# Attention and expert MLP on one core: another slot plan for the attention stage (turning point, projections, loads and low parts moved)

## The chip, the core and the metric

The kernel runs on one core of a Trainium2 chip, in one launch. The metric is the device time in microseconds of one execution. Engines: TensorE (PE), VectorE (DVE), ScalarE (ACT), GpSimd (POOL), and SyncE (SP), which here only issues DMAs. Each of them runs its own list of instructions in the order written; semaphores tie the lists together.

## The reference

`x` is 8 x 512 x 512 in float32. Two layers are added to it, one after the other:

```
query = seq2 + b_self;  key = concat(seq1 + b_prev, seq2 + b_self);  value = concat(seq1, seq2)
q, k, v = query @ Wq + bq, key @ Wk + bk, value @ Wv + bv        # 16 heads of 32
score_prev = mask(q . k[:l1]) * SCALE;  score_self = (q * k[l1:]).sum(-1) * SCALE
weights = softmax(concat(score_prev, score_self))
attn = weights[:-1] @ v[:l1] + weights[-1] * v[l1:]
x = x + (attn @ Wo + bo)                                          # seq1 = x, seq2 = fside
h = gelu(x @ W1 + b1)                                             # 512 -> 2048
x = x + concat(h @ W2 + b2, h @ We[expert] + be[expert])          # 384 + 128 columns
```

Each query sees the 512 keys of the other sequence, masked by a length, and one key of its own.

## The kernel before, in words

The program has two stages. The second is the output projection and the expert MLP; the change does not touch it. The first is the attention, and it runs over 8 batches b with 4 groups g of 4 heads each (128 of the 512 features). The first batch and the last are written out, the six between are one hardware loop.

A product of float32 precision is made of three matmuls: each operand is split into a high part, which the matmul takes as it is, and a low part that holds the rest (`in_hi`, `in_lo`, `w_hi`, `w_lo`). A projection of a group sums 12 such matmuls of 128x512 and is issued in three **thirds** of 4 matmuls. There are four of them per group: k, q, k2 (the key of the query's own position) and v2 (its value), in this order, thus 12 thirds, numbered 0 to 11.

For each group TensorE makes 16 **maximum tiles** (L1148: scores with a query on each partition; VectorE's L832 reduces a tile to a column of maxima), 16 **score tiles** (L1175: the same scores with a key on each partition and the maximum already subtracted; ACT's L639 exponentiates a tile into `p_f`), the sums over keys with the values (**value bursts**, L1188, four matmuls per tile row t of keys) and the denominators (L1197) from sums that POOL makes of the probabilities (L531 and L534, 12 of 128x512 per group).

The work is laid out by hand in 16 **slots** i of each group, one per score tile, and it is staggered. Beside the scores of group g, a slot holds maximum tiles of the next group (`tiles_of_max`) and thirds of the group after next (`thirds_of`). The tables `turn_at`, `in_hi_at` and `in_lo_at` say in which slot (g, i) of batch b an input block j of batch b+1 is transposed on DVE (L806), has its high part made on ACT (L582) and its low part on POOL (L539). Blocks 0 to 3 are of x, 4 to 7 of seq2. The loads that feed them (L317, four DMAs a block, 4 buffers) stand on SP. `turned` has two buffers, so transpose j waits for the low part of block j-2. The k projection of the next batch's group 0 (in group 2) waits for low parts 0 to 3, its q projection for all eight.

In slot 8 of group g TensorE issues the value bursts of tile rows 0 and 1, the denominators of the group before, the own scores (L1157) and the transposition of the maxima (L1165). From there a chain runs to the next group's first tiles: ACT copies the own scores (L622), DVE makes the maximum and its two parts (L840 to L855), SP writes these into the operand of the next group's scores (four DMAs, `stacks<-m_neg`, L339), and then SP writes the **stacks** of the group after next, the operands of its maximum tiles, from the parts of k and q (12 DMAs `stacks<-parts`, L332, three for each of four heads j, with one of the mask at L328 ahead of them where the group is 0 or 1). The first maximum tile in slot 0 of the next group waits for stack 0. SP takes, in each group, in this order: loads (in groups 0 and 1), m_neg of the next group, the stacks of the group after next, the own weights (L348) and the store of the group before (L353).

## Time and profile before

| | before |
|---|---|
| median of 3 runs | 1864.58 us (1861.9 to 1869.23) |
| the profiled execution | 1861.9 us |
| its span, from first to last instruction | 1860.1 us |
| VectorE, ScalarE, GpSimd busy | 49%, 38%, 34% of the span |
| mean granted TensorE clock | 0.968 |
| first stage | up to about 1035 us; one batch of the loop takes about 119 us |
| second stage | about 825 us |

Busy time counts a matmul from its start to the modelled end, so overlapping matmuls count once and short pauses vanish. Where the start times of neighbouring matmuls are farther apart than one matmul needs, TensorE waited. In a timeline, "x2" merges neighbours of one kind, and the brackets at the end tell how long the engine was idle before and who released it.

### The profile page before, as it was taken

The numbers are of one execution on the slowest core, as the hardware profiler recorded it, in microseconds if no ns is written. First come the engines' busy times: TensorE is split into PE (matmuls) and PEld (weight loads), VectorE is DVE, ScalarE is ACT, GpSimd is POOL, SyncE is SP. The second block draws the span as 40 slices with busy tenths as digits, with TensorE's granted clock in tenths as the row PEclk, the third lists the DMA queues.
The fourth block names the chain that finished last, engine by engine and source line by source line (L and its number), as shares of the span: only waits on it lengthen the run. The fifth ranks groups of instructions, "written<-read, shape, count | busy, mean of one in ns | idle before, by whom it ended". The sixth has DMA issues, their size and how long they took to land.

```text
span 1860.1 us, 27844 instructions
## 1 busy us (share of the span) xinstructions
PE 1757.1 (94%) x8384; PEld 1290.8 (69%) x8384; DVE 915.6 (49%) x1399; ACT 709.8 (38%) x1258; POOL 626.6 (34%) x489
## 2 busy tenths in 40 slices
PE   6999999999999999999995899999999999999997
PEld 5666656666566565666651688888888888888886
DVE  4567575775767757667586633222131323132311
ACT  3254353544545435444445242323232323333222
POOL 3167485665765748648375200000000000000000
PEclk8999999999999999999996899999999999999999
DMA  6452434424344335344243321313030312121101
GB/s 139 73 112 70 98 84 103 97 67 101 85 109 81 91 71 116 87 91 94 57 117 121 85 86 23 68 22 70 11 73 17 58 30 52 34 43 47 30 15 23
DMA packets 361052, 132.67 MB, mean 71 GB/s; under 512 B 288202, under 2 KB 328138, under 8 KB 360978
## 3 DMA queue, kind: packets, MB, share of 16 engines
q1 hardware_dynamic: 356370, 129.75, 31.9%
q10 hardware_dynamic: 4608, 2.10, 0.4%
q8 instruction: 26, 0.43, 0.1%
q14 instruction: 48, 0.39, 0.1%
HBM read 62.02 MB, written 18.89 MB: 44 GB/s over the span
## 4 chain that ended last, share of the span: by engine, by line
PE 73%; SPq 7%; issue 6%; DVE 4%; DMA 4%; POOL 4%; ACT 1%; POOLq 0%; DVEq 0%; ACTq 0%
PE ps_proj L1117 10%; PE ps_av L1069 6%; PE ps_av L1071 6%; PE ps_av L1070 6%; PE ps_max L1148 6%; PE ps_av L1188 5%; PE ps_score L1175 3%; DMA stacks<-parts 3%; PE ps_proj L1069 3%; PE ps_max L1071 3%; PE ps_score L1071 3%; PE ps_max L1070 3%; PE ps_score L1070 3%; PE ps_score L1069 3%; PE ps_max L1069 3%
## 5 line engine op out<-in xcount | busy, mean ns | idle before, releaser
L639 ACT ACTIVATE p_f<-ps_score 128x512 f32<-128x512 f32 x512 | 304.9, 599 | 462.2 <-PE ps_score L1175 436.4
L832 DVE TENSOR_REDUCE m_col<-ps_max 128x1 f32<-128x512 f32 x512 | 329.1, 683 | 230.4 <-PE ps_max L1148 229.2
L534 POOL TENSOR_TENSOR p_sum<-p_sum,p_f 128x512 f32<-128x512 f32 x256 | 338.8, 1355 | 2.7 <-ACT p_f L639 2.7
L1002 DVE TENSOR_TENSOR h_lo<-h_f,h_hi 128x512 fp32r<-128x512 f32 x128 | 88.3, 690 | 481.1 <-ACT h_hi L729 480.9
L531 POOL TENSOR_TENSOR p_sum<-p_f 128x512 f32<-128x512 f32 x128 | 162.9, 1304 | 228.1 <-PE ps_av L1197 224.0
L1175 PE MATMUL ps_score<-stacks 99*128 99x512 f32 x512 | 212.3, 425 | 20.0 <-ACT p_f L639 19.9
L1117 PE MATMUL ps_proj<-in_hi,w_hi 128*128 128x512 f32 x512 | 208.6, 407 | 18.0 <-POOL in_lo L539 14.7
L1148 PE MATMUL ps_max<-stacks 97*128 97x512 f32 x512 | 188.1, 435 | 39.0 <-DMA stacks<-parts 28.3
L1117 PE MATMUL ps_proj<-in_lo,w_hi 128*128 128x512 f32 x512 | 206.4, 403 | 0.0
L1117 PE MATMUL ps_proj<-in_hi,w_lo 128*128 128x512 f32 x512 | 205.9, 402 | 0.0
L1069 PE MATMUL ps_av<-y_hi,w_hi 128*128 128x512 f32 x512 | 199.4, 390 | 1.3 <-DVE y_lo L998 1.3
L1071 PE MATMUL ps_av<-y_hi,w_lo 128*128 128x512 f32 x512 | 199.3, 389 | 0.0
L1070 PE MATMUL ps_av<-y_lo,w_hi 128*128 128x512 f32 x512 | 199.2, 389 | 0.0
L727 ACT ACTIVATE h_f<-ps_av,bias 128x512 f32<-128x512 f32 x128 | 88.2, 689 | 242.9 <-PE ps_av L1071 216.8
L1148 PEld LDWEIGHTS ps_max<-stacks 97*128 97x128 f32 x512 | 98.1, 195 | 107.6 <-DVE m_col L832 56.1
L729 ACT ACTIVATE h_hi<-ps_av,bias 128x512 fp32r<-128x512 f32 x128 | 88.2, 689 | 209.0 <-PE ps_max L1071 209.0
L1175 PEld LDWEIGHTS ps_score<-stacks 99*128 99x128 f32 x512 | 98.4, 193 | 84.7 <-issue 38.1
L1188 PE MATMUL ps_av<-p_f,v_st 128*32 128x512 f32 x1024 | 131.3, 627 | 2.6 <-ACT p_f L639 2.6
L1117 PEld LDWEIGHTS ps_proj<-in_hi,w_hi 128*128 128x128 f32 x512 | 100.1, 195 | 41.4 <-POOL in_lo L539 9.1
L1117 PEld LDWEIGHTS ps_proj<-in_lo,w_hi 128*128 128x128 f32 x512 | 99.9, 195 | 21.9
L1117 PEld LDWEIGHTS ps_proj<-in_hi,w_lo 128*128 128x128 f32 x512 | 99.5, 194 | 21.7
L892 DVE RECIPROCAL den<-den 128x128 f32<-128x128 f32 x128 | 112.2, 918 | 0.8
(116 smaller groups left out, 2657.7 us busy)
## 6 DMA issues: line engine op xcount, KB each, us to landing
stacks<-parts SPq DMA_DIRECT2D x384, 128.0 KB
raw<-in_x_dram SPq DMA_DIRECT2D x128, 64.0 KB, 2.2
raw<-in_fside_BxSxS_dram SPq DMA_DIRECT2D x128, 64.0 KB, 2.2
den<-own_scratch SPq DMA_DIRECT2D x128, 64.0 KB, 2.7
attn_scratch<-num SPq DMA_DIRECT2D x32, 256.0 KB, 2.9
x_raw<-in_x_dram SPq DMA_DIRECT2D x128, 64.0 KB, 2.2
a_raw<-attn_scratch SPq DMA_DIRECT2D x32, 256.0 KB, 3.5
we_raw<-in_L_cond_We_dram SPq DMA_DIRECT2D x32, 256.0 KB, 2.7
```

The lines of the kernel that those rows point to most:

```text
L531: pool.tensor_tensor(p_sum[:, j], p_f[:, j], now, ALU.add).then_inc(sum_made, 1)
L534: pool.tensor_tensor(p_sum[:, j], p_sum[:, j], now, ALU.add).then_inc(sum_made, 1)
L639: act.activation(p_f[:, i % FLIGHT], ps_score[i % 2][:, :], ACT.Exp, scale=SCALE).then_inc(p_made, 1)
L832: dve.tensor_reduce(m_col[:, n % C, n // C:n // C + 1], ps_max[n % 2][:, :], AX.X, ALU.max).then_inc(max_made, 1)
L892: dve.reciprocal(den[:, r, at], den[:, r, at]).then_inc(rden_made, 1)
L1069: pe.matmul(ps, left[0], right[0], start=first, stop=False)
L1070: pe.matmul(ps, left[0], right[1], start=False, stop=False)
L1071: return pe.matmul(ps, left[1], right[0], start=False, stop=last)
L1117: mm = pe.matmul(ps, left, right, start=(m == 0), stop=(m == 3 * C - 1))
L1148: pe.matmul(ps_max[n % 2][:, :], q_st[0:KM, r, j, P * t:P * (t + 1)], k_st[0:KM, r, j, :], start=True, stop=True).then_inc(max_mm, 1)
L1175: pe.matmul(ps_score[i % 2][:, :], k_st[0:KS, r, j, P * t:P * (t + 1)], q_st[0:KS, r, j, :], start=True, stop=True).then_inc(score_mm, 1)
L1188: pe.matmul(ps_num[at, :], v_st[:, t, P * g + DH * j:P * g + DH * (j + 1)], p_f[:, i % FLIGHT], start=(t == 0), stop=(t == C - 1)).then_in ...
```

## The change

The slot tables of the attention stage are replaced. The maximum tiles are spread over slots 0 to 9 and not 0 to 7. The value bursts of rows 0 and 1, the denominators and the turning of the maxima, with the steps of ACT and DVE that follow, move from slot 8 to slot 9 (on ACT and DVE from 9 to 10), POOL's sums one slot later too. The thirds stand in other slots. The transposes and the high and low parts of the next batch's inputs stand later in group 1 and group 2. The loads of x move from the start of group 0 to the start of group 1, and those of seq2 from the start of group 1 to behind the m_neg DMAs of group 1, eight ahead of stack 0 and eight ahead of stack 2. In DVE's slot 10 `own_max` now stands ahead of `q_low`. Nothing is computed otherwise, and no instruction is added or taken away.

```diff
@@ -239,15 +239,15 @@
 
         def tiles_of_max(i):
 
-            ends = (2, 4, 6, 8, 10, 12, 14, TILES)
+            ends = (2, 3, 5, 7, 8, 10, 12, 14, 14, TILES)
             return range(ends[i - 1] if i else 0, ends[i]) if i < len(ends) else range(0)
 
 
 
-        turn_at = {(1, 3): (0,), (1, 4): (1,), (1, 7): (2,), (1, 8): (3,), (1, 11): (4,), (1, 12): (5,),
-                   (2, 1): (6,), (2, 2): (7,)}
-        in_hi_at = {(1, 5): (0,), (1, 6): (1,), (1, 8): (2,), (1, 9): (3,), (1, 15): (4,), (2, 0): (5,), (2, 2): (6,), (2, 3): (7,)}
-        in_lo_at = in_hi_at
+        turn_at = {(1, 6): (0,), (1, 7): (1,), (1, 11): (2,), (1, 12): (3,), (1, 14): (4,), (1, 15): (5,),
+                   (2, 2): (6,), (2, 3): (7,)}
+        in_hi_at = {(1, 10): (0,), (1, 11): (1,), (1, 12): (2,), (1, 13): (3,), (2, 0): (4,), (2, 2): (5,), (2, 4): (6,), (2, 5): (7,)}
+        in_lo_at = {(1, 10): (0,), (1, 11): (1,), (1, 12): (2,), (1, 13): (3,), (2, 0): (4,), (2, 2): (5,), (2, 4): (6,), (2, 5): (7,)}
 
 
 
@@ -273,11 +273,11 @@
 
         def thirds_of(g, i):
 
-            slots = ((4, 5, 5, 6, 7, 7, 9, 10, 11, 12, 13, 14), (0, 2, 3, 4, 5, 6, 9, 10, 11, 12, 13, 14),
-                     (0, 2, 3, 5, 6, 7, 9, 10, 11, 12, 13, 15), (0, 2, 3, 4, 5, 6, 9, 10, 11, 12, 13, 15))[g]
+            even = (0, 2, 3, 4, 6, 7, 8, 10, 11, 12, 14, 15)
+            slots = (range(4, TILES), even, (0, 2, 3, 7, 8, 10, 11, 12, 13, 14, 15, 15), even)[g]
             return [n for n, at in enumerate(slots) if at == i]
 
-        k_at, q_at = (6, 4, 4, 4), (8, 7, 8, 7)
+        k_at, q_at = (7, 4, 4, 4), (10, 8, 11, 8)
 
         def first_max(t):
 
@@ -402,8 +402,8 @@
             def batch(b, first, last):
                 for g in range(C):
                     more = not (last and g >= 2)
-                    if g < 2 and not last:
-                        for j in range(C * g, C * (g + 1)):
+                    if g == 1 and not last:
+                        for j in range(C):
                             load(b + 1, j)
                     if last and g == 2:
                         for n in range(6):
@@ -412,6 +412,9 @@
                         maxima(*after(b, g, 1))
                     if more:
                         for j in range(HG):
+                            if g == 1 and j % 2 == 0 and not last:
+                                load(b + 1, C + j)
+                                load(b + 1, C + j + 1)
                             stack(*after(b, g, 2), j)
                     if last and g == 2:
                         for n in range(6, 10):
@@ -557,14 +560,14 @@
                                 in_low(b + 1, j)
                         if i == 8:
                             own_value(b, g)
-                        n = (i + 7) % TILES
-                        if i >= 9:
+                        n = (i + 6) % TILES
+                        if i >= 10:
                             add_probabilities(b, g, 1 + n // HG, n % HG)
                         elif n < SUMS and not (first and g == 0):
                             add_probabilities(*after(b, g, -1), 1 + n // HG, n % HG)
 
             batches(pool, batch)
-            for n in range(7, SUMS):
+            for n in range(6, SUMS):
                 add_probabilities(B - 1, C - 1, 1 + n // HG, n % HG)
 
         @block.scalar
@@ -678,7 +681,7 @@
                     project = not (last and g >= 2)
                     maximum = not (last and g == C - 1)
                     for i in range(TILES):
-                        if i == 9 and maximum:
+                        if i == 10 and maximum:
                             maxima_twice(*nxt)
                             own_row(*nxt)
                         if i == 15 and maximum:
@@ -944,17 +947,18 @@
                                 maximum(*nxt, n)
                         if i == 3 and started:
                             numerator(*after(b, g, -1))
-                        if i == 10 and started:
+                        if i == 11 and started:
                             denominator(*after(b, g, -1))
                         if not last:
                             for j in turn_at.get((g, i), ()):
                                 turn(b + 1, j)
                         if i == k_at[g] + 1 and project:
                             k_low(*nxt2)
+                        if i == 10 and bound:
+                            own_max(*nxt)
                         if i == q_at[g] + 1 and project:
                             q_low(*nxt2)
-                        if i == 9 and bound:
-                            own_max(*nxt)
+                        if i == 10 and bound:
                             m_parts(*nxt)
                             own_less_max(*nxt)
                         if i in (13, 14) and started:
@@ -1235,12 +1239,12 @@
                         if i == 1 and not (first and g == 0):
                             for t in (2, 3):
                                 value_burst(*after(b, g, -1), t)
-                        if i == 8:
+                        if i == 9:
                             for t in (0, 1):
                                 value_burst(b, g, t)
                             if not (first and g == 0):
                                 denominators(*after(b, g, -1))
-                        if bound and i == 8:
+                        if bound and i == 9:
                             own_scores(*nxt)
                             turn_max(*nxt)
             batches(pe, batch)
```

SP in group 1 of batch 0, before: L348 fetches own weights, L317 loads inputs, L339 writes m_neg, L332 the parts into a stack.

```order
L348 DMA den<-own_scratch 32x4x128 x4
L317 DMA raw<-in_fside_BxSxS_dram 32x16x32 x16
L339 DMA stacks<-m_neg 2x4x128 x4
L332 DMA stacks<-parts 32x1024
L332 DMA stacks<-parts 32x2x512 x2
```

And now:

```order
L348 DMA den<-own_scratch 32x4x128 x4
L317 DMA raw<-in_x_dram 32x16x32 x16
L339 DMA stacks<-m_neg 2x4x128 x4
L317 DMA raw<-in_fside_BxSxS_dram 32x16x32 x8
L332 DMA stacks<-parts 32x1024
L332 DMA stacks<-parts 32x2x512 x2
L332 DMA stacks<-parts 32x1024
L332 DMA stacks<-parts 32x2x512 x2
L317 DMA raw<-in_fside_BxSxS_dram 32x16x32 x8
L332 DMA stacks<-parts 32x1024
L332 DMA stacks<-parts 32x2x512 x2
```

Eight loads stand between m_neg and stack 0 and eight between stacks 1 and 2; the sixteen at the start are those of x.

POOL from group 1 to the own value of group 2 in batch 0, before: L539 makes a low part of an input, L522 multiplies an own value, L531 and L534 are the sums of probabilities.

```order
L539 TENSOR_TENSOR in_lo<-turned,in_hi 128x512 x3
L522 TENSOR_TENSOR v<-v,den 128x512
L539 TENSOR_TENSOR in_lo<-turned,in_hi 128x512
L531 TENSOR_TENSOR p_sum<-p_f 128x512 x4
L534 TENSOR_TENSOR p_sum<-p_sum,p_f 128x512 x2
L539 TENSOR_TENSOR in_lo<-turned,in_hi 128x512
L534 TENSOR_TENSOR p_sum<-p_sum,p_f 128x512
L539 TENSOR_TENSOR in_lo<-turned,in_hi 128x512
L534 TENSOR_TENSOR p_sum<-p_sum,p_f 128x512 x2
L539 TENSOR_TENSOR in_lo<-turned,in_hi 128x512
L534 TENSOR_TENSOR p_sum<-p_sum,p_f 128x512
L539 TENSOR_TENSOR in_lo<-turned,in_hi 128x512
```

And now, from the fifth low part on (ahead of these rows stand the own value and, four times in turn, one low part and one first sum, L542 and L534):

```order
L537 TENSOR_TENSOR p_sum<-p_sum,p_f 128x512 x2
L542 TENSOR_TENSOR in_lo<-turned,in_hi 128x512
L537 TENSOR_TENSOR p_sum<-p_sum,p_f 128x512 x2
L542 TENSOR_TENSOR in_lo<-turned,in_hi 128x512
L537 TENSOR_TENSOR p_sum<-p_sum,p_f 128x512 x2
L542 TENSOR_TENSOR in_lo<-turned,in_hi 128x512
L537 TENSOR_TENSOR p_sum<-p_sum,p_f 128x512
L542 TENSOR_TENSOR in_lo<-turned,in_hi 128x512
L537 TENSOR_TENSOR p_sum<-p_sum,p_f 128x512
L525 TENSOR_TENSOR v<-v,den 128x512
```

Before, three low parts stand ahead of the own value and one ahead of the first sum, and between the first sum and the last low part stand 10 sums. Now all eight stand behind the own value, with 11 sums ahead of the last of them.

## Rows read from the trace of the kernel before

**Rows 1.** The page, part 1: busy time, share of the span, instructions.

```profile
PE 1757.1 (94%) x8384; PEld 1290.8 (69%) x8384; DVE 915.6 (49%) x1399; ACT 709.8 (38%) x1258; POOL 626.6 (34%) x489
```

**Rows 2.** Windows: stretch, length, busy time of each engine, PEclk, DMA share, GB/s.

```profile
541.80:660.70 118.90, 112.45 (x593) 74.67 (x592) 81.58 (x129) 54.68 (x105) 77.02 (x61) 0.99 0.41 91
...
1035.40:1860.10 824.70, 811.29 (x3585) 672.01 (x3584) 225.21 (x331) 251.30 (x389) 0.00 (x0) 0.99 0.21 44
```

**Rows 3.** Timeline of PE: start, length, engine, line, operation; two scores a slot apart.

```profile
457.34 0.40 PE L1175 MATMUL ps_score<-stacks 99*128 99x512 f32 x1
...
458.50 0.40 PE L1175 MATMUL ps_score<-stacks 99*128 99x512 f32 x1
```

**Rows 4.** Timeline of PE: the turning points of groups 0, 1, 2, 3 and 0.

```profile
452.26 0.40 PE L1165 MATMUL ps_max<-ident,m_col 128*8 128x128 f32 x8
...
478.22 0.40 PE L1165 MATMUL ps_max<-ident,m_col 128*8 128x128 f32 x8
...
508.62 0.40 PE L1165 MATMUL ps_max<-ident,m_col 128*8 128x128 f32 x8
...
534.07 0.40 PE L1165 MATMUL ps_max<-ident,m_col 128*8 128x128 f32 x8
...
571.17 0.40 PE L1165 MATMUL ps_max<-ident,m_col 128*8 128x128 f32 x8
```

**Rows 5.** The chain that ended last, 534 to 544: start, length, what.

```profile
535.79 0.69 SPq L339
...
539.12 0.57 SPq L332
...
543.09 0.48 PE ps_max L1148
```

**Rows 6.** Timeline of PE, group 2: first maximum tiles, first third of q.

```profile
487.79 0.69 PE L1148 MATMUL ps_max<-stacks 97*128 97x512 f32 x2 [1.54 <-DMA stacks<-parts]
...
499.63 0.50 PE L1117 MATMUL ps_proj<-in_hi,w_hi 128*128 128x512 f32 x1 [1.50 <-POOL in_lo L539]
```

**Rows 7.** Timeline of POOL: the fourth and the eighth low part.

```profile
480.42 1.29 POOL L539 TENSOR_TENSOR in_lo<-turned,in_hi 128x512 fp32r<-128x512 f32 x1
...
498.28 1.29 POOL L539 TENSOR_TENSOR in_lo<-turned,in_hi 128x512 fp32r<-128x512 f32 x1
```

**Rows 8.** Timeline of ACT: a cast to in_hi; the probability behind a turning point.

```profile
473.42 0.61 ACT L582 CAST in_hi<-turned 128x512 fp32r<-128x512 f32 x1
...
509.64 0.60 ACT L639 ACTIVATE p_f<-ps_score 128x512 f32<-128x512 f32 x1 [0.51 <-PE ps_score L1175]
```

**Rows 9.** Timeline of SP: loads and m_neg in group 1, loads in group 0.

```profile
469.90 10.89 SPq L317 DMA_DIRECT2D raw<-in_fside_BxSxS_dram  x16
480.84 2.68 SPq L339 DMA_DIRECT2D stacks<-m_neg  x4
...
551.50 8.45 SPq L317 DMA_DIRECT2D raw<-in_x_dram  x16
```

**Rows 10.** Waits, 300 to 1000: who for whom, us in total, times, longest.

```profile
PEld ps_max L1148 <- DVE m_col L832: 41.1, 118, 0.9
```

**Rows 11.** Lines L810 (q_low) and L898 (normalization): ns min/median/max, first and last start.

```profile
L810 DVE TENSOR_TENSOR parts<-q_f,parts x32: 648/692/716, 37.0 to 952.7; 128x512 fp32r<-128x512 f32 x32
...
L898 DVE TENSOR_TENSOR num<-num,den x32: 692/1526/1753, 126.3 to 1049.2; 128x512 f32<-128x512 f32 x32
```

**Rows 12.** Windows behind two waits: PEclk is the third number from the end.

```profile
499.70:503.50 3.80, 3.80 (x10) 2.98 (x11) 1.26 (x2) 0.60 (x1) 3.57 (x3) 0.55 0.00 0
...
663.90:667.30 3.40, 3.39 (x8) 2.71 (x9) 1.34 (x2) 1.57 (x3) 3.40 (x4) 0.50 0.76 175
```

**Rows 13.** Timelines of POOL and PE at the end of the first stage.

```profile
1016.07 5.87 POOL L531 TENSOR_TENSOR p_sum<-p_f 128x512 f32<-128x512 f32 x4 [14.53 <-PE ps_av L1197]
...
1034.46 1.04 PE L1197 MATMUL ps_av<-p_sum,ones 128*32 128x512 f32 x2 [0.63 <-POOL p_sum L534]
```

## The prediction, made before the changed kernel was run

> **What bounds the kernel now.** Read the share of busy time first, then doubt it: TensorE is busy for 94% of the span [rows 1], but the windows show that the idle part lies in the first stage. One batch of the loop, 541.8 to 660.7, leaves it 6.5 us by the profile's count, while the whole second stage of 825 us loses 13 [rows 2]. The busy share hides more, since matmul records overlap. Two scores that stand a slot apart, with one third of a projection between them, start 1.16 us apart [rows 3]: five matmuls, 0.23 each. A third costs 0.93, a score or a maximum tile 0.23.
>
> The useful mark in this stage is the "turning point": the start of the matmuls L1165, which turn the maxima. Call the one in group g T_g. They stand at 452.26, 478.22, 508.62, 534.07 and 571.17 [rows 4], so the steps are T0 to T1 25.96, T1 to T2 30.40, T2 to T3 25.45, T3 to the next T0 37.10, 118.9 us a batch. From each of them a chain runs that TensorE can't shorten. From 534.07: SyncE starts the four m_neg DMAs at 535.79, starts the stacks of the group after at 539.12, and TensorE's first maximum tile starts at 543.09 [rows 5]: 9.02 us. Beside this chain TensorE has only what stands between the turning point and the end of the group: 7 scores and 6 thirds, 7.2 us. So it waits at each group's start. What stands behind the turning point in a group is free up to about 9 us; what stands ahead of it is paid in full. That is the rule by which I cost the moves.
>
> Group 1 to group 2 is the longest step for its work. The first tile comes at 487.79, 9.57 after T1, with a wait of 1.54; at 499.63 the first third of q waits for POOL's in_lo [rows 6]. POOL had run without a gap from 480.42 until the eighth in_lo ended at 499.57, 15 operations (10 sums, 5 in_lo), 1.277 each [rows 7]. The first three in_lo lay before that, while POOL was idle anyway.
>
> **The change, part by part.** *Turning point one slot later, in every group.* In groups 0, 1 and 3 seven scores and six thirds stood behind it. Now six scores stand there, with six thirds in group 0 (0.23 us less cover), five in groups 1 and 3 (1.16 less), seven in group 2 (0.70 more). What leaves the cover goes ahead of the next mark of its own group, so the step that ends in that group grows: T0 to T1 by 1.16, T2 to T3 by 1.16, T3 to T0 by 0.23.
>
> *in_lo moved behind the marks.* POOL's 8 in_lo now all stand behind the denominators of group 1, with 11 sums among and ahead of the last: 19 operations, not 15. The first can't start before ACT's probability of slot 10, which starts 1.0 after a mark (509.64 against 508.62) and takes 0.60, and a cast to in_hi of 0.61 [rows 8]: T1 + 2.2. So the last in_lo ends at 2.2 + 19 x 1.277 = T1 + 26.5. q's first third is moved from slot 5 to 7 of group 2, but it needs all eight. TensorE's own work up to there is only about 16 us in both kernels, so this wait grows and is not covered. In the kernel before it took 508.62 - 499.63 = 8.99 from that third to T2 [rows 4, 6]; now one third, one score and two maximum tiles fewer stand in between (1.63): 7.4. T1 to T2 is then 33.9 against 30.40: +3.5.
>
> *Loads moved.* SyncE's sixteen loads at the start of group 1 took 10.89 us, because they waited for transposes, and the m_neg DMAs came right behind them, at 480.84, 0.9 later than they otherwise would [rows 5, 9]. That 0.9 goes: the loads at the start of group 1 are now those of x, for which nothing is awaited; such sixteen took 8.45, 0.53 each [rows 9]. But eight loads now stand ahead of stack 0 and eight ahead of stack 2. Stack 0 starts at T1 + 1.72 + 2.7 + 8 x 0.53 + 0.5 of waits = 9.1, and by rows 5 its tile starts 3.97 later: T1 + 13.1, not 9.57. TensorE will stand there some 6.9 us. Does that add to the POOL wait? Both lie between T1 and the same third. From 13.1, the work of slots 0 to 6 and the start of 7 is 9.5, hence 22.6, and stack 2 comes at 4.2 + 1.9 + 4.2 + 1.9 behind the start of stack 0, so tile 8 can't start before about 21.8 and VectorE's reductions of tiles 8 to 11, 0.65 each, with k_low between, bring the third to about 26. POOL's 26.5 is later by little. I charge the larger, not both. Behind the waiting stacks are own_weights and the store of the attention; their users come in slot 8 and later.
>
> *Turns.* Turn j waits for in_lo j-2. On VectorE, behind turns 2 to 5 of group 1, stand the reciprocals, qk, the normalization and the next group's maxima. The in_lo 0 to 3 end at T1 + 3.5, 6.0, 8.6, 11.1, so the normalization ends about 13.8, when the first tile comes anyway: nothing charged, up to 1 us in the upper end.
>
> *Maximum tiles spread.* In slots 5 to 7 of groups 1 and 3 two tiles each now meet a slot without a third, so VectorE (1.3 us for two) is briefly the slower; on the other side the turns leave slots 3 and 4. TensorE's weight loads wait for reductions 118 times in 700 us, 41 us in all [rows 10], but much of it lies beside a running matmul. I take +0.2 for each of groups 1 and 3, between -1.1 (the largest part of such waits in group 1 gone) and +1.
>
> *q_low later.* In group 2 q is cast in slot 11, so q_low ends about T2 + 4.6 on VectorE, and the first parts DMA of stack 0, which waits for it and has a mask DMA of 0.3 ahead, could start at 5.0 [rows 5]. All q_low of the kernel before took 0.65 to 0.72, at a time when POOL is mostly idle; the normalization, also two SBUF inputs, took 0.69 at best and 1.53 in the median, with POOL at its sums [rows 11]. q_low will now meet the sums. The stack comes between 0 and 1.2 later; I take 0.5 on T2 to T3. The Trainium skill, page "SBUF — State Buffer", section "SBUF: two separate sides", says that a VectorE operation with two SBUF inputs and a GpSimd operation exclude each other for the whole instruction. By that rule q_low would always wait for a sum, and the step would be at the upper end, 1.2.
>
> *The clock.* After the wait for in_lo the granted clock was 0.55 over 499.7 to 503.5, the 1.2 GHz level for most of it; in batch 5, after the wait at the start of group 0, it was 0.50 for 663.9 to 667.3 [rows 12]. 3.4 us at half the rate lose 1.7. Group 3 now gives 1.16 less cover before exactly this place, so it will fall more often: +0.3 in the mean, up to 1.6. The loss after in_lo is in the 7.4 already. The Trainium skill, page "TensorE: Matmul & The Clock Gate", section "Part 1: The HAM clock gate", says that idling throttles the array and activity releases it; by it the long stop at group 2's first tile brings a further half-rate stretch. Its 1 to 2 us would lie ahead of POOL's 26.5, where they are hidden.
>
> **The sum.** Per batch 1.36 + 3.5 + (1.16 + 0.2 + 0.5) + (0.23 + 0.3) = 7.3. Loads and group 2's projections exist in seven of the eight batches: 51. In the last batch T0 to T1 adds 1.2. At its end POOL's twelve last sums run from 1016.07 and TensorE's last denominator waits for them [rows 13]; they start one slot later, where scores come every 1.0 us: +1.0. Sum 53.4. The profiled execution took 1861.9 (span 1860.1), so 1915; it was the fastest of the three, the median is 1864.6.
>
> **Rivals.** *Only the later mark costs* (0.12). If POOL's wait and SyncE's stop are hidden, T1 to T2 stays at 30.4: 3.8 x 7 + 2.2 = 29, 1891. For it: POOL is idle a third of each step. Against: its idle time lies before the denominators, and the in_lo were taken out of it.
>
> *The waits add up* (0.11). If the stop at stack 0 and its half-rate stretch push TensorE behind POOL, q's third comes at 29 (T1 to T2 +6.2), q_low takes its 1.2, and every group 0 meets the slow clock (+1.6): about 12 a batch, 1947.
>
> *Faster: the in_lo wait goes* (0.06). q's third is two slots later. If the last in_lo were ready by T1 + 17, the 2.0 us before 499.63, the slow clock behind it (1.4), the 0.9 of SyncE and the 0.7 of cover in group 2 would all be won: 5.1; with group 1's waits for reductions gone too (1.1 instead of +0.2), a batch gets 7.3 - 3.5 - 5.1 - 1.3 = 2.6 shorter, 1846. It decides at T1 + 17, and 19 POOL operations can't be done by then.
>
> *Balance* (0.05). Half of that gain meets the later mark: within 0.5%, which is 9 us and about what a measurement of this kernel can tell from no change.
>
> **How the numbers follow.** My own case has 0.66, with 1903 to 1929 as its range. Its 1915 is the forecast. The lower rival at 1891 is taken in, of the upper one the nearer half: 1889 to 1940. Faster 0.06, same 0.05, slower 0.89.
>
> **What would show it.** In the profile after: the maximum tile at group 2's start about 13 us behind its mark, released by a stack DMA; sixteen x loads without a wait, then eight loads between m_neg and the stacks; POOL without a gap for 24 us in front of q's first third, which waits for in_lo; T0 to T1 about 27.3, T1 to T2 34, T2 to T3 27.3, T3 to T0 37.6; a second stage unchanged at 825. I am wrong if T1 to T2 is at 31 or below, or if steps T0 to T1 and T2 to T3 don't grow by about one slot.

## The result and the profile after

The changed kernel takes 1949.41 us (median of 4 runs, 1937.86 to 1966.88) against 1864.64 before: a ratio of 1.046, with a 95% interval of 1.037 to 1.055. It is slower, as forecast, but by 85 us and not by 53. 1949 lies outside the range of 1889 to 1940. One execution among the experiments below (e1's of 1980.38 us) is over 1.5% slower than the fastest of its kernel, in a slower state of the chip, and is left out of the medians and ratios. In its profiled execution (1959.29 us, span 1957.5) the first line of the page, which answers to [rows 1], reads:

```profile
PE 1794.4 (92%) x8384; PEld 1305.5 (67%) x8384; DVE 937.5 (48%) x1399; ACT 711.9 (36%) x1258; POOL 628.1 (32%) x489
```

TensorE has the same 8384 matmuls and more busy microseconds for them, and VectorE has 22 us more busy time for the same 1399 instructions. Both are explained below. The windows (columns as in [rows 2]) show one batch, from turning point to turning point, and the second stage:

```profile
624.06:753.91 129.85, 116.20 (x600) 75.90 (x592) 83.08 (x128) 54.90 (x104) 77.47 (x60) 0.96 0.38 84
1132.80:1957.50 824.70, 811.27 (x3585) 671.78 (x3584) 225.19 (x331) 251.44 (x389) 0.00 (x0) 0.99 0.21 44
```

The second stage still takes 824.7 us, to the tenth. All of the loss is in the first stage: 129.9 a batch and not 118.9, in a batch without any special event. The turning points of this batch, on TensorE's timeline, answer to [rows 4] (T0, T1, T2, T3 and the next T0; all line numbers are three or four higher now):

```profile
624.06 0.40 PE L1169 MATMUL ps_max<-ident,m_col 128*8 128x128 f32 x8
...
651.47 0.40 PE L1169 MATMUL ps_max<-ident,m_col 128*8 128x128 f32 x8
...
687.68 0.40 PE L1169 MATMUL ps_max<-ident,m_col 128*8 128x128 f32 x8
...
716.49 0.40 PE L1169 MATMUL ps_max<-ident,m_col 128*8 128x128 f32 x8
...
753.91 0.40 PE L1169 MATMUL ps_max<-ident,m_col 128*8 128x128 f32 x8
```

Taken over the whole profiled execution, the steps add up so ("usual" is the value that most batches share; the excess is measured minus before, summed over all such steps):

| step | before | forecast | usual after | others after | excess in all |
|---|---|---|---|---|---|
| T0 to T1 (8) | 25.95 | 27.3 | 27.42 | 31.90 once | 16.9 |
| T1 to T2 (7) | 30.4 | 33.9 | 34.8 to 36.3 | 40.16, 40.87 | 47.7 |
| T2 to T3 (7) | 25.45 | 27.3 | 28.80 | none | 23.4 |
| T3 to T0 (7) | 37.1 or 38.8 | 37.6 | 37.4 or 39.1 to 40.0 | none | 7.3 |
| T1 to T2, last batch | 25.48 | | 27.84 | | 2.4 |

The sum is 97.7, the difference of the two spans 97.4. T1 to T2 holds half of it. The forecast had 53.4 in all; of the 44 beyond it T1 to T2 (with the last batch) makes 26, T2 to T3 10, T0 to T1 6 (4.5 of it in one batch) and T3 to T0 4; the rest of the stage gives 1 to 2 back. Three things happen in the first stage that the prediction priced too low or not at all; the first two lie in T1 to T2.

*First: TensorE stands for stack 0, and then POOL stands too.* In batch 4 the timelines of TensorE, ScalarE and POOL (start, length, engine, line, operation, idle time before it and who ended it) show behind T1 = 651.47:

```profile
664.29 1.19 PE L1152 MATMUL ps_max<-stacks 97*128 97x512 f32 x2 [4.31 <-DMA stacks<-parts]
...
667.98 3.01 PE L1192 MATMUL ps_av<-p_f,v_st 128*32 128x512 f32 x16
...
676.62 0.50 PE L1152 MATMUL ps_max<-stacks 97*128 97x512 f32 x1 [1.23 <-DVE m_col L835]
...
679.16 1.09 PE L1152 MATMUL ps_max<-stacks 97*128 97x512 f32 x2 [0.52 <-DVE m_col L835]
680.33 0.70 PE L1121 MATMUL ps_proj<-in_hi,w_hi 128*128 128x512 f32 x1
```

```profile
672.10 0.61 ACT L585 CAST in_hi<-turned 128x512 fp32r<-128x512 f32 x1
```

```profile
672.79 1.30 POOL L542 TENSOR_TENSOR in_lo<-turned,in_hi 128x512 fp32r<-128x512 f32 x1 [2.58 <-ACT in_hi L585]
...
679.00 1.27 POOL L542 TENSOR_TENSOR in_lo<-turned,in_hi 128x512 fp32r<-128x512 f32 x1
```

The first maximum tile comes at T1 + 12.8 (forecast 13.1). q's first third comes at 680.33, which is T1 + 28.9 and not 26.5. POOL was not gapless: its sixth low part waited 2.58 us for a cast that stands in ScalarE's order behind a probability, and this behind a score that TensorE held back. TensorE's own tiles ahead of the third are done at 680.25, 0.08 before it, so POOL's low part (ended 680.27) and TensorE's chain arrive there together, and both had been held by the stop. From q's third to T2 it is 7.35 (forecast 7.4).

*Second: a VectorE instruction of 7.11 us.* In batch 3 VectorE's timeline reads as follows, with those of POOL and TensorE behind it:

```profile
528.73 0.65 DVE L809 STREAM_TRANSPOSE turned<-raw 128x512 f32<-128x512 f32 x1
529.30 7.11 DVE L901 TENSOR_TENSOR num<-num,den 128x512 f32<-128x512 f32 x1
536.34 1.27 DVE L835 TENSOR_REDUCE m_col<-ps_max 128x1 f32<-128x512 f32 x2
```

```profile
532.12 1.30 POOL L542 TENSOR_TENSOR in_lo<-turned,in_hi 128x512 fp32r<-128x512 f32 x1
533.35 2.52 POOL L537 TENSOR_TENSOR p_sum<-p_sum,p_f 128x512 f32<-128x512 f32 x2
542.84 1.29 POOL L542 TENSOR_TENSOR in_lo<-turned,in_hi 128x512 fp32r<-128x512 f32 x1 [6.98 <-ACT in_hi L585]
```

```profile
537.07 0.79 PE L1152 MATMUL ps_max<-stacks 97*128 97x512 f32 x1 [3.34 <-DVE m_col L835]
```

The normalization reads two tensors of SBUF. POOL had worked without a gap since 519.78 and stopped at 535.87; the normalization ended 0.54 us later, at 536.41. The maxima's reductions stood behind it and TensorE behind them. The same happened in batch 6 (40.87). In the other batches it took 0.90 to 0.98 us, from the same place.

*Third: q_low.* The two lines that answer to [rows 11] (minimum/median/maximum of 32, in ns):

```profile
L813 DVE TENSOR_TENSOR parts<-q_f,parts x32: 680/688/1851, 37.1 to 1047.8; 128x512 fp32r<-128x512 f32 x32
```

```profile
L901 DVE TENSOR_TENSOR num<-num,den x32: 691/1482/7111, 130.8 to 1145.8; 128x512 f32<-128x512 f32 x32
```

In groups 0 and 2, where q_low now meets POOL's sums, it takes 1.55 and 1.65. The median of 688 hides that, as 18 of the 32 still take 0.68 to 0.73.

The clock, in windows around the stop at stack 0 and around q's third (PEclk is the third number from the end):

```profile
663.40:670.20 6.80, 5.91 (x20) 3.08 (x24) 2.75 (x4) 0.60 (x1) 6.80 (x6) 0.50 0.79 146
670.20:680.40 10.20, 8.09 (x34) 4.46 (x26) 8.70 (x15) 5.54 (x10) 7.62 (x8) 1.00 0.48 126
680.50:683.90 3.40, 3.40 (x9) 2.63 (x10) 0.48 (x1) 0.60 (x1) 2.24 (x2) 0.50 0.00 0
```

TensorE is granted the 1.2 GHz level for 6.8 us from the end of the stop on and again for 3.4 us behind q's third. The value burst at 667.98 falls into the first and takes 3.01 us; at the full rate it takes 1.92. In batch 2 the first stretch (397.1 to 404.0) is over when the burst starts at 403.71; the burst takes 2.03, and q's third comes at T1 + 27.9 and not 28.9. In the seven steps T1 to T2 the half rate holds for 85 us in all, where it held for 27 before; in the whole execution it is 207 and 120. Most of TensorE's added busy time is there.

### The profile page after: what moved, and what is told of

The parts are those of the page before. It is cut to its first block, busy times and chain, and to the rows that moved or that the text cites. A ratio compares the mean times of both kernels' runs of the same rounds, so it can differ in the third digit from the quotient of the medians.

```text
span 1957.5 us, 27844 instructions
## 1 busy us (share of the span) xinstructions
PE 1794.4 (92%) x8384; PEld 1305.5 (67%) x8384; DVE 937.5 (48%) x1399; ACT 711.9 (36%) x1258; POOL 628.1 (32%) x489
## 4 chain that ended last, share of the span: by engine, by line
PE 67%; issue 10%; SPq 6%; DMA 5%; DVE 5%; POOL 4%; ACT 1%; POOLq 0%; DVEq 0%; ACTq 0%
PE ps_proj L1121 8%; PE ps_av L1073 6%; PE ps_av L1074 6%; PE ps_av L1075 6%; PE ps_max L1152 5%; PE ps_av L1192 4%; PE ps_proj L1073 3%; DMA stacks<-parts 3%; PE ps_proj L1074 3%; PE ps_proj L1075 3%; PE ps_max L1074 3%; PE ps_score L1074 3%; PE ps_max L1073 3%; PE ps_score L1073 3%; PE ps_max L1075 3%
## 5 line engine op out<-in xcount | busy, mean ns | idle before, releaser
L1152 PE MATMUL ps_max<-stacks 97*128 97x512 f32 x512 | 200.1, 445 | 99.0 <-DMA stacks<-parts 68.7
L534 POOL TENSOR_TENSOR p_sum<-p_f 128x512 f32<-128x512 f32 x128 | 166.9, 1328 | 253.9 <-PE ps_av L1201 251.7
L1179 PE MATMUL ps_score<-stacks 99*128 99x512 f32 x512 | 217.3, 431 | 27.4 <-ACT p_f L642 27.4
L1121 PE MATMUL ps_proj<-in_hi,w_hi 128*128 128x512 f32 x512 | 213.7, 417 | 11.2 <-POOL in_lo L542 7.6
L1192 PE MATMUL ps_av<-p_f,v_st 128*32 128x512 f32 x1024 | 141.7, 669 | 1.8 <-ACT p_f L642 1.8
L542 POOL TENSOR_TENSOR in_lo<-turned,in_hi 128x512 fp32r<-128x512 f32 x64 | 82.1, 1284 | 120.3 <-ACT in_hi L585 120.3
```

What stands on the lines that cost most here:

```text
L534: pool.tensor_tensor(p_sum[:, j], p_f[:, j], now, ALU.add).then_inc(sum_made, 1)
L1121: mm = pe.matmul(ps, left, right, start=(m == 0), stop=(m == 3 * C - 1))
L1152: pe.matmul(ps_max[n % 2][:, :], q_st[0:KM, r, j, P * t:P * (t + 1)], k_st[0:KM, r, j, :], start=True, stop=True).then_inc(max_mm, 1)
L1179: pe.matmul(ps_score[i % 2][:, :], k_st[0:KS, r, j, P * t:P * (t + 1)], q_st[0:KS, r, j, :], start=True, stop=True).then_inc(score_mm, 1)
L1192: pe.matmul(ps_num[at, :], v_st[:, t, P * g + DH * j:P * g + DH * (j + 1)], p_f[:, i % FLIGHT], start=(t == 0), stop=(t == C - 1)).then_in ...
```

## The experiments

Ten kernels were run, each beside the kernel before on the same chip. Slots are (group, slot). M0 is the first maximum tile behind a turning point.

### e1: the loads of blocks 4 and 5 ahead of the m_neg transfers

```diff
-                        for j in range(C):
+                        for j in range(C + 2):
                             load(b + 1, j)
-                            if g == 1 and j % 2 == 0 and not last:
+                            if g == 1 and j == 2 and not last:
```

> The changed kernel, with the loads of blocks 4 and 5 ahead of the m_neg DMAs of group 1 and no longer between these and stack 0 (6 and 7 stay ahead of stack 2). Theory (the two waits add up: the stop at stack 0 holds score 2, ACT's cast of block 5 stands behind that score's probability, and POOL starves for it): T1 to the first maximum tile falls from 12.8 to about 8.7, POOL runs without a gap, q's first third comes at T1 + 26.5, T1 to T2 is 34 and not 36.2, the 40 us cases go; about 25 us in all, near 1920. Rival (POOL's order alone makes the step): T1 to T2 stays at 36, and the time within 10 us of the changed kernel. The other steps stay at 27.4, 28.8 and 37.5 to 39.

Measured: 1943.22 (1940.94 to 1950.89), ratio 1.042 (1.037 to 1.047): 6 us below the changed kernel, not 25, and the intervals overlap. M0 comes at T1 + 8.6: the stop is gone. But T1 to T2 is 33.9 in batch 4, only 2.4 less than in the changed kernel, and 34.1 in batch 6. In batch 4 POOL has no gap and q's third waits for its last low part, at T1 + 26.5, as forecast. The median does not gain even 2.4 a batch, since three batches have a normalization of 7.1 us and steps of 40.4 to 41.9. So two bounds, about 2 us apart, lie side by side in this step; taking the longer away uncovers the other.

### e2 and e3: the change in two halves

e2 is the changed kernel with the loads and the tables of transposes and parts of before. What is left is the later mark, with the thirds and tiles of the change. e3 is the other half: the kernel before with the loads and these tables of the change. The core of e3 as a diff to before:

```diff
-        turn_at = {(1, 3): (0,), (1, 4): (1,), (1, 7): (2,), (1, 8): (3,), (1, 11): (4,), (1, 12): (5,),
-                   (2, 1): (6,), (2, 2): (7,)}
+        turn_at = {(1, 6): (0,), (1, 7): (1,), (1, 11): (2,), (1, 12): (3,), (1, 14): (4,), (1, 15): (5,),
+                   (2, 2): (6,), (2, 3): (7,)}
...
+                            if g == 1 and j % 2 == 0 and not last:
+                                load(b + 1, C + j)
+                                load(b + 1, C + j + 1)
```

> The changed kernel with the loads and the tables of transposes, high and low parts as they were before; the later turning point, the thirds, the maximum tiles and the steps tied to them stay. What is left is the slot shift alone. Theory: T0 to T1 27.4, T2 to T3 28.8 and T3 to T0 37.5 as in the changed kernel, but T1 to T2 falls below the 30.4 of before, to about 27, because only 13 POOL operations stand between the turning point and the last in_lo, and q's first third stands two slots later; about 1 us a batch over the kernel before, near 1872. Rival (the later mark makes most of the loss): over 1900.

> The kernel before with the loads and the tables of transposes, high and low parts of the changed one; turning point, thirds and maximum tiles as before. Theory: T0 to T1 26.0, T2 to T3 25.5 and T3 to T0 37 to 38.8 as before, T1 to T2 from 30.4 to 35 to 38, since 20 POOL operations and the stop at stack 0 lie ahead of q's third; 1897 to 1915. Rival (these moves cost only beside the later mark): below 1880.

Measured: e2 1897.09 (1891.3 to 1911.02), ratio 1.017 (1.013 to 1.021); e3 1917.88 (1910.45 to 1929.23), ratio 1.029 (1.024 to 1.035). Over the 1862.77 of before in that job the halves cost 34 and 55 us, 89 together, against 85 for the whole, so they hardly work on each other. e2 had been expected near 1872, with over 1900 as the rival; it lies close to the rival. The later mark costs about 5 us more than the forecast's rival of the mark alone (29), although T1 to T2 is not 30.4 there, as that rival had it, but 28.1 to 28.8 in five of seven batches and 30.0 in two (about 27 expected). T0 to T1 is 27.9 and T2 to T3 28.8. The latter is as in the whole change, so the excess there belongs to the mark (q_low's later slot goes with it). In e3 T0 to T1 is 25.1, 0.9 less than before: TensorE's waits for VectorE in this step, 1.1 in all, are down to 0.2, which fits the transposes that left slots 3 and 4. The prediction had this gain only as the far end (-1.1) of a term that it took at +0.2. T1 to T2 is 38.0 to 38.6, a little above the 38 expected, and 44.8 where the normalization took 7.09; the time is 3 us above the 1915 at the upper end.

### e4: q_low with one operand from PSUM

```diff
-                dve.tensor_tensor(q_lo[:, :], q_f[:, :], f(q_hi[:, :]), ALU.subtract)
+                dve.scalar_tensor_tensor(out=q_lo[:, :], in0=ps_proj[0][:, :], scalar=bias[:, 0, c:c + 1],
+                                         in1=f(q_hi[:, :]), op0=ALU.add, op1=ALU.subtract)
```

> The changed kernel with q_low made from PSUM (projection plus bias minus the high part), as k_low is, so that this VectorE operation reads one operand of SBUF only and not two. Theory (an operation with two SBUF inputs waits for POOL's running sum): q_low in groups 0 and 2 falls from 1.55 to 1.65 to about 0.7, T2 to the first maximum tile from 10.24 to about 9.3, T2 to T3 from 28.8 to about 27.9, the rest unchanged: 6 us in all. Rival (the length comes from elsewhere, such as the order behind own_max): q_low stays at 1.6 and nothing moves.

Measured: 1954.25 (1953.34 to 1955.92), ratio 1.049 (1.045 to 1.053): no gain, where 6 us were expected. The local reading is right. The line of q_low, which answers to the one of 680/688/1851:

```profile
L813 DVE SCALAR_TENSOR_TENSOR parts<-ps_proj,bias,parts x32: 740/747/753, 37.1 to 1045.3; 128x512 fp32r<-128x512 f32 x32
```

M0 moves from T2 + 10.24 to T2 + 9.5, and T2 to T3 is 28.05 in most batches. But twice the normalization behind T2, which had never been long, now took 6.84 us and the step 34.7, and once the one behind T1 took 7.10. The next experiments ask whether these long instructions are a cause or a mark.

### e5 and e6: the normalization with one operand from PSUM

e6 is the changed kernel with this alone. e5 has it together with e1 and e4.

```diff
-                dve.reciprocal(den[:, r, at], den[:, r, at])
+                dve.reciprocal(ps_den[:, at], den[:, r, at])
...
-                dve.tensor_tensor(num[:, r], num[:, r], den[:, r], ALU.mult)
+                dve.tensor_tensor(num[:, r], num[:, r], ps_den[:, :], ALU.mult)
```

> The changed kernel with the normalization's reciprocal read from PSUM, and nothing else. Theory of starvation by POOL: the normalization takes .7 to 1.0 us everywhere, T1->T2 is 35 to 36.2 in all seven batches and never 40; 10 to 15 us below the changed kernel, 1930 to 1938. Rival (another cause): one to three T1->T2 at 40 to 41 remain, the time within 5 us of the changed kernel.

> The changed kernel with the loads of blocks 4 and 5 ahead of the m_neg transfers, and with both VectorE operations that read two SBUF tensors (q_low and the normalization) reading one of them from PSUM. Theory (VectorE starves while POOL runs without a gap, and the stop at stack 0 costs what the loads behind m_neg cost): no normalization over 1.5 us, q_low at .75, T1->T2 33.9 in all seven batches, T2->T3 28.0, T0->T1 27.4; about 7 x (1.5 + 3.5 + 2.6 + 1) = 60 above the 1863 of before, 1920 to 1925. Rival (the long normalizations only mark a disturbance that has another cause): some T1->T2 stay at 40 and the time at 1940 to 1950.

Measured: e6 1940.64 (1939.28 to 1941.58), ratio 1.042 (1.038 to 1.046), 9 us below the changed kernel. The line of the normalization in e6:

```profile
L901 DVE TENSOR_TENSOR num<-num,ps_av x32: 647/686/689, 130.6 to 1127.8; 128x512 f32<-128x512 f32 x32
```

T1 to T2 is 34.5 to 36.4 in all seven batches, never 40 (the two intervals overlap, so the verdict rests on the steps). Not all of the gain is the long instruction's: in four batches the step is 34.5 to 34.9 where the changed kernel mostly has 36.2. In batch 4, for one, the half-rate stretch behind the stop begins at T1 + 9.5 and not 11.9, and it is over when the value burst starts. The long normalizations were a cause of the steps of 40. In the profiles of the kernels with both operands in SBUF there were ten of them (two after, three in e1, one each in e2 and e3, three in e4), of 6.84 to 8.88 us. In each one POOL's gapless run had begun 6.5 to 9.5 us before it, and each ended 0.54 or 0.55 us after this run's last operation.

e5: 1929.52 (1927.09 to 1931.98), ratio 1.036 (1.032 to 1.040); expected 1920 to 1925. T0 to T1 27.3, T1 to T2 33.0 to 34.0 in six of seven batches (35.2 in the first), T2 to T3 28.05: all three nearly as expected. T3 to T0 is 38.6 to 40.2, in the mean 1.6 more than in the kernel before, where 1 was assumed. In e5 the bound of POOL that the prediction worked out stands alone in batches 4 and 6; in most others POOL has a gap of 0.7 to 1.1. T1 of batch 4 is 637.39, POOL has no gap, and its last low part and q's first third are:

```profile
661.90 1.29 POOL L542 TENSOR_TENSOR in_lo<-turned,in_hi 128x512 fp32r<-128x512 f32 x1
```

```profile
663.24 0.80 PE L1122 MATMUL ps_proj<-in_hi,w_hi 128*128 128x512 f32 x1
```

T1 + 25.8, where the prediction had 26.5.

### e7: one third from slot 4 to slot 5 in groups 1 and 3

```diff
-            even = (0, 2, 3, 4, 6, 7, 8, 10, 11, 12, 14, 15)
+            even = (0, 2, 3, 5, 6, 7, 8, 10, 11, 12, 14, 15)
```

> The changed kernel with one third moved in groups 1 and 3 from slot 4 to slot 5. Theory (the wait of .94 + .23 us of TensorE for the maxima's reductions in slots 6 and 7 comes of too little work of TensorE in the slots ahead of it): M0->T0 and M0->T2 shorter by .8 each, 14 x .8 = 11 us below the changed kernel, about 1935. Rival (it is VectorE that is behind by the sum of its work): no change within 3 us.

Measured: 1936.05 (1929.96 to 1938.5), ratio 1.039 (1.035 to 1.043). T0 to T1 is 27.0 and T2 to T3 28.4: each 0.4 shorter, not 0.8. The waits of 0.94 and 0.23 in slots 6 and 7 became one of 0.74 in slot 5. So about 6 us of the 13 belong to the third's place; the profiled execution also had no long normalization. The time is as expected, but by luck: the steps moved by half of what the theory said. The place of the third decides over a third of this wait; what makes the rest was not tested.

### e9: the cast one slot earlier

e6 with one more edit, aimed at POOL's gap of 2.58 us.

```diff
-        in_hi_at = {..., (2, 0): (4,), (2, 2): (5,), (2, 4): (6,), (2, 5): (7,)}
+        in_hi_at = {..., (2, 0): (4,), (2, 1): (5,), (2, 4): (6,), (2, 5): (7,)}
```

> The changed kernel with the normalization's reciprocal read from PSUM (so that the long normalizations are absent), and ScalarE's cast of x's high part 5 one slot earlier, in slot (2,1) ahead of probability 2 instead of (2,2) behind it. Theory (the stop at stack 0 holds score 2, probability 2, this cast and so POOL's low part 5, 1.9 us of POOL's work): POOL's gap ahead of low part 5 is gone, q's first third comes 1.9 us earlier, T1->T2 32.6 to 34 instead of 34.5 to 36.4, 7 x 1.9 = 13 us below the 1940.6 of the same kernel with the cast in its place, about 1927. Rival (the third waits for something else, or POOL is late in any case): T1->T2 and the time within 3 us.

Measured: 1936.72 (1936.15 to 1937.68), ratio 1.039 (1.034 to 1.044), 4 us below e6, not 13. T1 to T2 is 34.5 in most batches, as in e6. The gap in front of the sixth low part is gone (one of 1.4 stands ahead of the seventh) and POOL is done 0.4 earlier, but q's third is not. POOL and TensorE of batch 4, with T1 = 640.31 and M0 = 653.15:

```profile
666.27 1.27 POOL L542 TENSOR_TENSOR in_lo<-turned,in_hi 128x512 fp32r<-128x512 f32 x1
```

```profile
664.36 0.50 PE L1152 MATMUL ps_max<-stacks 97*128 97x512 f32 x1 [1.20 <-DVE m_col L835]
...
666.89 1.39 PE L1152 MATMUL ps_max<-stacks 97*128 97x512 f32 x2 [0.52 <-DVE m_col L835]
668.09 0.63 PE L1121 MATMUL ps_proj<-in_hi,w_hi 128*128 128x512 f32 x1
```

The last low part ends at 667.54, the third starts at 668.09, T1 + 27.8, exactly as in e6. So my theory of POOL's gap fell. What decides is the way from M0 to the third: 14.9 us of TensorE's slots 0 to 6 and of its waits for VectorE's reductions.

### e8 and e10: a version from what was learnt

Both are the kernel before, with the mark left in slot 8, more thirds behind it, the low parts of blocks 6 and 7 earlier, the load of block 7 later (ahead of stack 2), and both VectorE operations with an operand from PSUM. e10 differs from e8 in one place:

```diff
-            slots = ((4, 5, 5, 6, 7, 7, 9, 10, 11, 12, 13, 14), (0, 2, 3, 4, 5, 6, 9, 10, 11, 12, 13, 14),
-                     (0, 2, 3, 5, 6, 7, 9, 10, 11, 12, 13, 15), (0, 2, 3, 4, 5, 6, 9, 10, 11, 12, 13, 15))[g]
+            most = (0, 2, 3, 4, 5, 9, 10, 11, 12, 13, 14, 15)
+            slots = ((4, 5, 5, 6, 7, 9, 10, 11, 12, 13, 14, 15), most,
+                     (0, 2, 3, 6, 7, 9, 10, 11, 12, 13, 14, 15), most)[g]   # e8: (0, 2, 3, 7, 9, 9, 10, ...)
```

> A version built on the kernel before: the mark stays in slot 8, but more thirds stand behind it (seven instead of four to five, in the slots in which TensorE waits for the maximum's way round), x's low parts 6 and 7 one group earlier, the loads 4 to 6 at the start of group 1, q_low and the normalization with one operand from PSUM. Theory (what stands between the mark and the turning point is what TensorE waits with, and more of it shortens the stop): T0->T1 25.0, T1->T2 24.5, T2->T3 24.5, T3->T0 36.2, 110 a batch instead of 118.9, about 1805. Rival (the first slots, now bare, wait for ScalarE's and VectorE's rows by as much): within 1% of before.

> The version with more cover, in group 2 with one third each in slots 6, 7 and 9 instead of one in 7 and two in 9. Theory (in slots 4 to 8 of group 2 TensorE idled while it waited for maxima's reductions, and its clock fell to one half for the 3.4 us ahead of the turning point): no half-rate stretch in group 2, T1->T2 26.5 to 27.5 instead of 28 to 29.5, 7 x 1.5 = 10 us below 1849, about 1839. Rival (q's first third waits for x's low part 7 in slot 6 as it did in the kernel before): T1->T2 28 or more.

Measured: e8 1849.35 (1844.18 to 1850.08), ratio 0.992 (0.989 to 0.995); e10 1833.59 (1833.44 to 1837.18), ratio 0.984 (0.980 to 0.989). e8 gave 0.8% and not the 3% expected: T0 to T1 stayed at 26.1 and T2 to T3 is 26.1 (25.0 and 24.5 expected), T1 to T2 is 28.0 to 29.6 (24.5 expected); only T3 to T0 came at its 36.2. In e8's group 2 TensorE idled in slots 5 to 7 and fell to the half rate just ahead of T2:

```profile
611.00:614.50 3.50, 2.98 (x7) 2.13 (x7) 2.35 (x4) 0.60 (x1) 3.44 (x3) 0.57 0.00 0
```

In e10 one batch (turning point to turning point) reads:

```profile
554.45:668.96 114.51, 111.98 (x601) 73.57 (x594) 78.68 (x128) 54.48 (x104) 75.12 (x60) 1.00 0.43 95
```

The granted clock is 1.00 over the whole batch; T1 to T2 is 26.6 to 26.8 in six of the seven batches (28.0 in batch 6, with a half-rate stretch) where it was 30.4, and the batch 114.5 where it was 118.9. e10 is the fastest version here. One of its edits is separated: from e8 to e10 the thirds 3, 4 and 5 of group 2 stand in slots 6, 7 and 9 and not in 7, 9 and 9, so that one third's work goes from behind the mark to slots in which TensorE idled. T1 to T2 falls by 1.5 and T2 to T3 from 26.1 to 25.5, 16 us by the medians; why T2 to T3 falls too is open. How the rest is shared among the other edits is open. The thirds that were moved behind the mark in groups 1 and 3 shortened neither T0 to T1 (26.1, before 26.0) nor T2 to T3 (25.5, before 25.4).

## Why the prediction was right and wrong

*Direction and main rule: right.* The rule "what stands ahead of the mark is paid, what stands behind it is free" held. T0 to T1 grew by 1.46 (forecast 1.36), the first tile of group 2 came at T1 + 12.8 (13.1), the way from q's third to T2 was 7.35 (7.4), and the second stage did not change.

*The step that failed: "I charge the larger, not both".* For T1 to T2 the prediction set two bounds side by side, POOL's at T1 + 26.5 and TensorE's behind the stop at about 26, and took the larger. POOL's was good (25.8 in e5, where it stands alone). The other was 1.8 us too early: T1 + 27.8 in e6 and e9, and 28.9 in the changed kernel's batch 4, where the half-rate stretch caught the value burst. From M0 to the third it takes 14.9, not 13. The prediction counted TensorE's work (9.5) and VectorE's reductions apart and had the reductions run on. VectorE's timeline of e6, batch 4 (T1 = 643.33), shows that they don't:

```profile
662.41 1.29 DVE L835 TENSOR_REDUCE m_col<-ps_max 128x1 f32<-128x512 f32 x2 [1.83 <-PE ps_max L1152]
663.61 0.70 DVE L809 STREAM_TRANSPOSE turned<-raw 128x512 f32<-128x512 f32 x1
664.24 1.25 DVE L835 TENSOR_REDUCE m_col<-ps_max 128x1 f32<-128x512 f32 x2
665.41 0.68 DVE L866 TENSOR_TENSOR num<-ps_av,v 128x512 f32<-128x512 f32 x1
666.01 0.69 DVE L809 STREAM_TRANSPOSE turned<-raw 128x512 f32<-128x512 f32 x1
666.62 1.95 DVE L835 TENSOR_REDUCE m_col<-ps_max 128x1 f32<-128x512 f32 x3
```

VectorE idled for 1.83 us while TensorE did a value burst, and then had seven reductions, two transposes and an addition in a row, for which TensorE waited 1.2, 0.2 and 0.5. Tile 8 started at T1 + 22.4, not far from the forecast's 21.8, but its reduction only at 23.9. The second failure in the same step is that POOL was taken as gapless: the stop also held the casts back, so that in the changed kernel POOL's last low part came at T1 + 28.8 in batch 4 and not at 26.5. e9 shows that its gap is not what decides: with the low parts done earlier the third stays at 27.8. The statement that the half-rate stretch "would lie ahead of POOL's 26.5, where they are hidden" failed with it: once TensorE is the later one, nothing is hidden. The rival "the waits add up" had this mechanism (the third at 29, T1 to T2 +6.2), with 0.11. Its total of 1947 is close to 1949, yet only partly for its reasons: not every group 0 met the slow clock, and the next term was in no case at all.

*The term that was missing: the long normalization.* The prediction charged nothing for VectorE's normalization and read 1.53 and at most 1.75 from [rows 11]. In the changed kernel it begins inside a gapless run of POOL, and there it can take 7.1. In the profiled execution two of these add 4 to 5 us each to T1 to T2; by the medians e6, which has none, is 9 us faster than the changed kernel. The Trainium skill, page "SBUF — State Buffer", section "SBUF: two separate sides", says that of a VectorE operation with two SBUF inputs and a GpSimd operation that reads SBUF the one that starts first gets the shared pair of ports for its whole instruction and the other one blocks. The trace agrees as to which operations are struck and that a PSUM operand frees them (e4, e6). But one blocked turn behind an operation of 1.27 us would give about 2 us, and the trace has 7.11, as if the operation lost several turns in a row.

*Terms that were mis-sized.* VectorE's wait in group 3: forecast +0.2, measured 0.25 before (0.17 and 0.08 in slots 5 and 7) and 1.17 after: +0.92. In group 1 it hardly moved (1.14 before, 1.17 after; +0.2 forecast). q_low: forecast 0.5, measured 1.3 (M0 from 8.95 to 10.24), just above the upper end of 1.2 that was given for it. e4, in which the instruction takes 0.75, takes 0.74 of it away. The two make T2 to T3 28.8 and not 27.3: 10 us of the 32 that the forecast missed. The +1.0 at the end of the stage did not come: from the last turning point to the second stage's first matmul it is 55.5 us in both kernels.

*The clock.* T3 to T0 grew by 1.04 in the mean, where 0.23 for cover and 0.3 for the clock were forecast. The half-rate stretch in group 0 came in five of seven batches, and in three of seven before; at 1.6 a stretch (38.8 against 37.1 before) that makes 0.5 of it, by estimate. What makes the rest was not separated. Why it spares some batches is open; e5 has it in all, e8 and e10 in none.

## What to carry to other kernels

When two chains end at the same instruction, don't take the larger of two sums that were worked out apart: walk the slots behind the later start with every engine's queue in order, and let the price of the wait include a half-rate stretch. A VectorE operation with two SBUF inputs is not one with a fixed duration; look whether GpSimd works without a gap at its new place, and if it does, give the operation a PSUM operand. And the version that gained left the mark where it was. "Behind the mark is free" holds only while TensorE has work ahead of it: from e8 to e10 one third's work gained 16 us by going ahead of the mark, into slots in which TensorE idled.

## What the runs showed of the hardware

- A VectorE tensor_tensor of 128x512 with both inputs in SBUF takes 0.65 to 0.73 us alone, 0.80 to 1.85 beside GpSimd operations, and in ten cases 6.84 to 8.88 us, until 0.55 us after GpSimd's run of operations had ended. With the same start, 9.5 us into the run, it took 0.98 in one batch and 7.11 in another; what decides is open. With one input in PSUM it took 0.65 to 0.69 in all 32 cases.
- From the end of TensorE's stop of 4.3 us at stack 0 the granted clock was 0.50 for 6.8 us, and not for the 3.4 of [rows 12].
- T0 to T1 of batch 1 was 31.9 in the changed kernel and 29.9 to 32.5 in e2, e7 and e9, but 27.4 to 27.5 in e1, e4, e5 and e6. Packets of the instruction queues lie in this stretch, in e6 as well as in the changed kernel, so they alone don't explain it. The cause is open.
